# Mixture of experts by units of 256 rows, with the weights as stationary operand

## The chip, the cores and the metric

One core of a Trainium2 chip runs the kernel. The metric is device time in microseconds, the median of three runs: 465.23 us (462.66 to 465.39).

## The reference, cut to what matters

A cross attention with linear features, then a feed-forward mixture of eight experts, two for each row, over 2048 rows of 256 channels in fp32. The change touches the mixture alone.

```python
E, TOP_K, D, M = 8, 2, 256, 896
router_probs = softmax(layernorm(x) @ gate_w)
topk_w, topk_idx = top_k(router_probs, 2); topk_w /= sum(topk_w)
# rows sorted by expert, group_sizes rows for each of the 8
h = ragged_dot(rows, w1, group_sizes)                    # [n, 256] x [256, 896]
h = silu(h) * ragged_dot(rows, w3, group_sizes)
out_sort = ragged_dot(h, w2, group_sizes)                # [n, 896] x [896, 256]
x = x + sum over the two choices of topk_w * out_sort
```

## The kernel before, in words

**Attention, then the mixture.** The attention runs over eight pairs of 128 rows. Its last steps (`read`, `attend`, `project_attention`, the router of pairs 6 and 7) are interleaved with the mixture's first tiles. The router writes each normalised row twice, by an indirect DMA, into the `bucket` in HBM, a stretch of CAP rows for each expert, with its row number and weight behind it. The mixture then reads tiles of 128 rows from there.

**One tile.** (`mix` on the engines: L499, L855, L1082, L1339.) Each fp32 factor is held as two fp32r halves, and a product is hi*hi + hi*lo + lo*hi, so three matmuls. TensorE: `hidden` (L802) has the transposed rows as the stationary operand and streams 448 columns of the weights, 24 matmuls a tile for gate and up, in two halves c of the 896 channels; `x_transposes` (L783) turns the next tile's rows; `output` (L820) is the product with w2 of the tile before, 21 matmuls of 256 columns; `g_transposes` (L839) turns the gated channels, 7 of 128x128. ScalarE: `silus` (two of 448 columns), `evacuate_x`, `evacuate_y` (scaled by the row's weight), `load` (a register load of the row and the DMA of tile t+2), `high_g` (casts of the turned channels). VectorE: `gates` (product with the SiLU), `split_x`, `low_g` (the low halves). GpSimd: `add` (L489), an indirect DMA that adds the tile's rows to the output; each waits until the one before has landed.

**Weights.** w1, w3 and w2 of an expert are three DMAs of SyncE into one of two places of `raw`. In the first tile of expert e (table `tab_first`) the weights of e+1 are converted: `high_halves` (L1056) on ScalarE, three parts of two casts of 896 columns, and `low_part` (L485) on GpSimd, three subtractions. `expert_ready` counts experts and TensorE waits for it.

**Order of the tiles.** Four early tiles (`EARLY`, experts 0, 1, 1, 0) run before the counts are known. Then VectorE works out tables (which expert, which row, first of its expert, active or not) in small steps linked by `list_step` (L1445 to L1499), between its work for tiles 2 and 3. `tiles_of_mixture` (L198) runs tiles 5 to 7 written out, 8 to 31 in a loop of eight with a table value for the expert, and the rest under an If each. Engines read table values with `value_load`, a register load.

## Time and profile before

| | |
|---|---|
| three runs | 465.39, 462.66, 465.23 us |
| the profiled execution | 464.74 us, its span 463.0 us |
| granted TensorE clock, mean | 0.988 |
| busy: TensorE matmul, weight load | 428.7 us (93%), 396.0 us (86%) |
| busy: VectorE, ScalarE, GpSimd | 209.6 (45%), 230.9 (50%), 213.3 us (46%) |
| DMA | 46.1 MB, mean 100 GB/s |
| chain that ended last, by engine | PE 68%, DVE 9%, issue 6%, POOL 5%, DMA 4% |

The page tells busy shares of one execution. Starts of neighbouring instructions say more than their durations on TensorE, since matmuls overlap. Line numbers are those of the kernel above.

### The profile page before, as it was taken

Reading aid. Unit: us, or ns where it says so; the run is one execution under the profiler, and the core shown is the slowest. Engines: PE = TensorE matmul, PEld = TensorE weight load, DVE = VectorE, ACT = ScalarE, POOL = GpSimd, SP = SyncE. Lnnn points to the kernel's source line nnn. Section 1 sums busy time; section 2 is a strip of 40 time slices with the busy share of each in tenths; the row PEclk is TensorE's granted clock in tenths of the full one; section 3 lists DMA queues with packets and bytes.
Section 4 is the critical chain, followed back from the end, with each engine's and each line's share of the span. In section 5 each row is a group of like instructions: output and inputs, shape, how many; then the busy total and the mean of one; then the engine's idle time right before and its main releaser. Section 6 shows DMA issues by size and latency. Waiting matters only on the chain.

```text
span 463.0 us, 12218 instructions
## 1 busy us (share of the span) xinstructions
PE 428.7 (93%) x3921; PEld 396.0 (86%) x3922; DVE 209.6 (45%) x582; ACT 230.9 (50%) x477; POOL 213.3 (46%) x209
## 2 busy tenths in 40 slices
PE   3899999999999999989999998999999999999970
PEld 3789988898988888979999898899999899999970
DVE  4457788758876784323233331333232333233220
ACT  3677777578865523745333732553272373333320
POOL 4424375657434641798321671482177177121121
PEclk9999999999999999999999999899999999999996
DMA  8644121462128448335731236118121121121121
GB/s 255 195 134 156 47 70 48 145 234 70 49 59 286 114 128 260 80 122 168 256 54 24 37 110 187 23 35 272 23 43 29 23 39 30 23 46 23 36 37 11
DMA packets 34523, 46.10 MB, mean 100 GB/s; under 512 B 3488, under 2 KB 29344, under 8 KB 34464
## 3 DMA queue, kind: packets, MB, share of 16 engines
q1 hardware_dynamic: 22304, 31.82, 20.6%
q0 software_dynamic: 6576, 8.82, 11.3%
q10 hardware_dynamic: 5584, 4.76, 3.7%
q8 instruction: 27, 0.44, 0.4%
q14 instruction: 32, 0.26, 0.2%
HBM read 32.63 MB, written 12.76 MB: 98 GB/s over the span
## 4 chain that ended last, share of the span: by engine, by line
PE 68%; DVE 9%; issue 6%; POOL 5%; DMA 4%; ACT 2%; ACTq 1%; POOLq 1%; DVEq 0%
PE bank L814 28%; PE twin L833 15%; PE bank L852 4%; DMA out_rows<-qf,x_all 3%; POOL w_lo L486 3%; PE twin L667 3%; PE bank L547 3%; PE bank L548 2%; PE bank L549 2%; DVE w_lo L1229 2%; PE bank L593 2%; PE twin L679 2%; PE bank L571 2%; PE twin L792 1%; PE bank L610 1%
## 5 line engine op out<-in xcount | busy, mean ns | idle before, releaser
L496 POOL DMA_INDIRECT out_rows<-qf,x_all x35 | 54.6, 1559 | 147.4 <-ACT qf L1054 111.7
L814 PE MATMUL bank<-w_hi,c_hi 128*128 (+1 forms) x280 | 106.4, 380 | 3.8 <-issue 2.0
L814 PE MATMUL bank<-w_lo,c_hi 128*128 (+1 forms) x280 | 103.0, 368 | 0.0
L833 PE MATMUL twin<-w_hi,kv_halves 128*128 (+1 forms) x490 | 95.2, 286 | 2.9 <-DVE kv_halves L1335 2.4
L1329 DVE TENSOR_TENSOR x_all<-bank,x_all 128x448 f32<-128x448 f32 x70 | 43.4, 623 | 97.3 <-ACT x_all L1073 97.2
L486 POOL TENSOR_TENSOR w_lo<-raw,w_hi x18 | 76.0, 4422 | 12.8 <-ACT w_hi L1066 10.1
L1335 DVE TENSOR_TENSOR kv_halves<-bank,kv_halves 128x512 fp32r<-128x512 f32 x66 | 38.6, 623 | 93.9 <-ACT kv_halves L1078 93.9
L833 PEld LDWEIGHTS twin<-w_hi,kv_halves 128*128 128x128 f32 x490 | 77.5, 188 | 3.7 <-DVE kv_halves L1335 2.6
L814 PE MATMUL bank<-w_hi,c_lo 128*128 (+1 forms) x280 | 79.9, 367 | 0.0
L1073 ACT ACTIVATE x_all<-bank 128x448 f32<-128x448 f32 x70 | 37.8, 544 | 80.6 <-PE bank L814 70.1
L833 PE MATMUL twin<-w_lo,kv_halves 128*128 (+1 forms) x245 | 68.7, 280 | 0.0
L814 PEld LDWEIGHTS bank<-w_hi,c_hi 128*128 128x128 f32 x280 | 53.1, 190 | 9.6 <-issue 5.6
L814 PEld LDWEIGHTS bank<-w_hi,c_lo 128*128 128x128 f32 x280 | 52.9, 189 | 4.5
L814 PEld LDWEIGHTS bank<-w_lo,c_hi 128*128 128x128 f32 x280 | 53.3, 190 | 3.6
L1078 ACT CAST kv_halves<-bank 128x512 fp32r<-128x512 f32 x66 | 32.4, 540 | 29.6 <-PE bank L852 22.8
L1054 ACT ACTIVATE qf<-twin,x_all 128x256 f32<-128x256 f32 x35 | 16.6, 476 | 60.2 <-PE twin L833 60.2
L833 PEld LDWEIGHTS twin<-w_lo,kv_halves 128*128 128x128 f32 x245 | 46.3, 189 | 0.1
L428 POOL DMA_INDIRECT bucket<-rows,slot x32 | 36.8, 1150 | 16.2 <-DVE slot L1320 8.5
L852 PE MATMUL bank<-ident,x_all 128*128 128x128 f32 x233 | 32.4, 274 | 3.7 <-DVE x_all L1329 3.7
L1066 ACT CAST w_hi<-raw x36 | 32.0, 939 | 6.1 <-issue 4.3
L852 PEld LDWEIGHTS bank<-ident,x_all 128*128 128x128 f32 x233 | 26.2, 140 | 5.3 <-DVE x_all L1329 5.2
L379 POOL TENSOR_SCALAR rs<-mv 128x2 f32<-128x2 f32 (+2 forms) x12 | 2.8, 231 | 50.0 <-DVE mv L1193 33.7
(219 smaller groups left out, 703.4 us busy)
## 6 DMA issues: line engine op xcount, KB each, us to landing
raw<-in_w SPq DMA_DIRECT2D x24, 896.0 KB
x_all<-bucket ACTq DMA_DIRECT2D x31, 129.0 KB, 2.1
raw<-in_ctxT SPq DMA_DIRECT2D x8, 256.0 KB, 2.9
out_rows<-x_all SPq DMA_DIRECT2D x8, 256.0 KB, 2.1
bucket<-pad_rows SPq DMA_DIRECT2D x13, 129.0 KB, 2.4
x_all<-in_x SPq DMA_DIRECT2D x2, 512.0 KB, 6.4
x_all<-bucket SPq DMA_DIRECT2D x6, 129.0 KB, 2.7
x_all<-in_x SPq DMA_DIRECT2D x1, 768.0 KB, 6.3
```

Of the source, the lines that this page charges most:

```text
L428: pool.indirect_dma_start(out=bucket, out_offset=bass.IndirectOffsetOnAxis(ap=slot[:, o, k:k + 1], axis=0), in_=rows[i % 2][:, o, k, :], i ...
L486: return pool.tensor_tensor(w_lo[:, bass.ds(at + i * W13, W13)], raw[:, bass.ds(at + i * W13, W13)], w_hi[:, bass.ds(at + i * W13, W13)].b ...
L496: pool.indirect_dma_start(out=out, out_offset=bass.IndirectOffsetOnAxis(ap=x_in[:, v, D:D + 1].bitcast(U32), axis=0), in_=y[:, v, :], in_o ...
L814: last = nc.tensor.matmul(bank[b][:, 0:MC], stationary[:, k, :], w[:, bass.ds(at + (of + k * M + c * MC), MC)], start=(k == 0 and part == ...
L833: last = nc.tensor.matmul(bank[6][:, 0:D], stationary[:, k, :], w[:, bass.ds(at + (2 * W13 + k * D), D)], start=(k == 0 and part == 0 and ...
L852: last = nc.tensor.transpose(b[:, at:at + P], g[:, k * P:(k + 1) * P], ident[:])
L1054: nc.scalar.activation(y[:, v, :], bank[6][:, 0:D], ACT.Copy, scale=x_in[:, v, D + 1:ROW]).then_inc(y_ready, 1)
L1066: nc.scalar.copy(w_hi[:, bass.ds(at + of, PIECE)], raw[:, bass.ds(at + of, PIECE)]).then_inc(hi_ready, 1)
L1073: nc.scalar.activation(silu[:, c, :], bank[c][:, 0:MC], ACT.Silu).then_inc(silu_ready, 1)
L1078: nc.scalar.copy(g_hi[:, k:end, :].rearrange("p k n -> p (k n)"), b[:, 0:(end - k) * P]).then_inc(g_hi_ready, 1)
L1329: nc.vector.tensor_tensor(g[:, c * MC:(c + 1) * MC], bank[2 + c][:, 0:MC], silu[:, c, :], ALU.mult).then_inc(g_ready, 1)
L1335: nc.vector.tensor_tensor(g_lo[:, k:end, :].rearrange("p k n -> p (k n)"), b[:, 0:(end - k) * P], g_hi[:, k:end, :].rearrange("p k n -> p ...
```

## The change

A unit is now 256 rows, two tiles of 128 side by side (`o`), or a single tile where an expert has an odd number of tiles. The weights are the stationary operand: for each block c of 128 channels (7) `gate_up` gives gate and up for 256 rows, already with channels on the partitions, so nothing is turned. Both lie in one PSUM bank (`gate_bank(c)`, four in a ring). SiLU, product, cast and low half are made for each block, and `down` takes two row tiles of it as stationary operand, into one bank for y. In a single the moving operand is the high and the low half of the 128 rows side by side (256 columns), and VectorE adds the two results (`sums`). The early part has two units of two tiles. TensorE walks by expert: pairs under Ifs, from the fourth on in a loop, then the single under an If. The other engines walk units, all written out. x_in is one buffer, so row number and weight are copied out (`copy_meta`). `expert_ready` is split into `w13_ready` and `w2_ready`.

```diff
-EARLY = ((0, 0, 5), (1, 0, 5), (1, P, 5), (0, P, 6))
+TWO = 2 * P
+EARLY = ((1, 5), (0, 6))
-SURE = 2 * T // P
-MOST = SURE + E + AHEAD
-TILES = MOST + 2
+SURE = 2 * T // TWO
+MOST = SURE + E + 4
+UNITS = MOST + 2
+RING = 4
+UNITS_LISTED, ROWS_LISTED, ALL_LISTED = 6, 10, 14
...
+        def units_of_mixture(eng, step):
+            for t in range(AHEAD, SURE):
+                step(t)
+            def unit_if_used(t):
+                go = eng.value_load(tab_active[0:1, t:t + 1], min_val=0, max_val=1)
+                with eng.If(go):
+                    step(t)
+                    if t + 1 < MOST - 2:
+                        unit_if_used(t + 1)
+            unit_if_used(SURE)
...
+            sp.wait_ge(meta_ready, 2)
+            sp.dma_start(x_in[:, 0, :], bucket[TWO:TWO + P, :]).then_inc(x_in_loaded, 16)
+            sp.wait_ge(pad_stored[1], 16 * 2)
+            sp.wait_ge(list_ready, ROWS_LISTED)
+            at = sp.value_load(tab_row2[0:1, AHEAD:AHEAD + 1], min_val=0, max_val=PAD_AT)
+            sp.dma_start(x_in[:, 1, :], bucket[bass.ds(at, P), :]).then_inc(x_in_loaded, 16)
...
+                low_halves(0)
+                add_unit(t - 1, 0)
+                low_halves(1)
+                add_unit(t - 1, 1)
+                low_halves(2)
...
+            def gate_up(t, e, c, single=False):
+                if c == 0:
+                    pe.wait_ge(x_hi_ready, t + 1)
+                    pe.wait_ge(w13_ready, e + 1)
...
+                for i in range(2):
...
+                    if single:
+                        for k in range(KD):
+                            for w in (w_hi, w_lo):
+                                last = nc.tensor.matmul(out_ap, block(w, k), c_halves[:, :, k, 0:P],
+                                                        start=(k == 0 and w is w_hi), stop=(k == KD - 1 and w is w_lo))
+                        continue
+                    for k in range(KD):
+                        nc.tensor.matmul(out_ap, block(w_hi, k), x_hi[:, k, :], start=(k == 0), stop=False)
+                        nc.tensor.matmul(out_ap, block(w_lo, k), x_hi[:, k, :], start=False, stop=False)
...
+                    for k in range(KD):
+                        last = nc.tensor.matmul(out_ap, block(w_hi, k), x_lo[:, k, :], start=False, stop=(k == KD - 1))
+                last.then_inc(h_done, 1)
...
+            def unit(t, e, at_before, single=False):
...
+                gate_up(t, e, 0, single)
+                gate_up(t, e, 1, single)
+                down(t - 1, MB - 1, at_before)
+                gate_up(t, e, 2, single)
+                gate_up(t, e, 3, single)
+                first_down(t, e, tiles)
+                gate_up(t, e, 4, single)
+                down(t, 1, at, tiles)
+                x_transposes(t + 1)
+                gate_up(t, e, 5, single)
+                down(t, 2, at, tiles)
+                gate_up(t, e, 6, single)
+                for c in (3, 4, 5):
+                    down(t, c, at, tiles)
...
+            x_transposes(2)
+            down(1, 5, at1)
+            pe.wait_ge(list_ready, UNITS_LISTED)
+            for e in range(E):
+                of = e * NT + (3 if e < 2 else 1)
+                start = pe.value_load(tab_start[0:1, e:e + 1], min_val=AHEAD, max_val=MOST)
+                def pairs_if_listed(j):
+                    with pe.If(pe.value_load(tab_pairs[0:1, of + 2 * j:of + 2 * j + 1], min_val=0, max_val=1)):
+                        unit(start + j, e, (e if j else max(e - 1, 0)) % 2 * WALL)
+                        if j == 0:
+                            pairs_if_listed(1)
+                        else:
+                            with pe.If(pe.value_load(tab_pairs[0:1, of + 4:of + 5], min_val=0, max_val=1)):
+                                with pe.Fori(2, NT // 2 - (1 if e < 2 else 0)) as r:
+                                    with pe.If(pe.value_load(tab_pairs[0:1, bass.ds(2 * r + of, 1)], min_val=0, max_val=1)):
+                                        unit(start + r, e, e % 2 * WALL)
+                pairs_if_listed(0)
...
+            def load(t):
+                at = [act.value_load(tab[0:1, t:t + 1], min_val=0, max_val=PAD_AT) for tab in (tab_row, tab_row2)]
...
+                act.wait_ge(meta_ready, t)
+                for o in range(2):
+                    act.dma_start(x_in[:, o, :], bucket[bass.ds(at[o], P), :]).then_inc(x_in_loaded, 16)
...
+            def block_of(t, c):
+                silus(t, c)
+                high_g(t, c)
...
+            def mix(t):
+                first = None if t == AHEAD else act.value_load(tab_first[0:1, t:t + 1], min_val=0, max_val=1)
+                high_halves(first, t, 0)
+                block_of(t, 0)
+                block_of(t, 1)
+                evacuate_y(t - 1, (t - 1) % RING, (t - 1) % 2)
+                high_halves(first, t, 1)
+                block_of(t, 2)
+                block_of(t, 3)
+                high_halves(first, t, 2)
+                block_of(t, 4)
+                block_of(t, 5)
+                evacuate_x(t + 1)
+                block_of(t, 6)
+                copy_meta(t + 1)
+                if t == AHEAD:
+                    act.wait_ge(list_ready, ALL_LISTED)
+                    count.extend((units_used(act), last_places(act)))
+                load(t + 2)
...
+            def sums(t, c):
+                dve.wait_ge(h_done, MB * t + c + 1)
+                nc.vector.tensor_reduce(gate_bank(c)[:].rearrange("p (i k n) -> p i k n", i=2, k=2)[:, :, 0, :],
+                                        single_bank(c)[:].rearrange("p (i k n) -> p i n k", i=2, k=2), AX.X, ALU.add).then_inc(summed, 1)
...
+            def products(t, c, n=TWO):
+                dve.wait_ge(silu_ready, MB * t + c + 1)
+                nc.vector.tensor_tensor(product_in(c)[:, 0:n], product_in(c)[:, 0:n], silu[:, c % 2, 0:n], ALU.mult).then_inc(g_ready, 1)
...
+                with dve.If(single):
+                    sums(t, 0)
+                    for c in range(MB):
...
+                        products(t, c, P)
+                        if c + 1 < MB:
+                            sums(t, c + 1)
+                        low_g(t, c, P)
```

On ScalarE, before: the end of the second conversion in a tile (L1066 casts to w_hi), the second SiLU (L1073), the next tile's rows (L1048) and y (L1054).

```order
L1066 COPY w_hi<-raw 128x896
L1066 ISA
L1066 COPY w_hi<-raw 128x896
L1059 UNCONDITIONAL_BRANCH
L1073 ACTIVATE x_all<-bank 128x448 [waits h_done]
L1048 CAST c_hi<-twin 128x256 [waits xT_done]
L1054 ACTIVATE qf<-twin,x_all 128x256 [waits y_added,y_done]
L1034 TENSOR_LOAD kf
```

After: the end of the first conversion (L1127), then blocks 0 and 1 (L1136 SiLU, L1140 cast) and the two tiles of y (L1110).

```order
L1127 COPY w_hi<-raw 128x896
L1127 ISA
L1127 COPY w_hi<-raw 128x896
L1116 UNCONDITIONAL_BRANCH
L1136 ACTIVATE x_all<-bank 128x256 [waits summed,h_done]
L1140 CAST kv_halves<-bank 128x256 [waits g_ready]
L1136 ACTIVATE x_all<-bank 128x256 [waits summed,h_done]
L1140 CAST kv_halves<-bank 128x256 [waits g_ready]
L1110 ACTIVATE qf<-twin,meta 128x256 [waits y_added,y_done]
L1110 ACTIVATE qf<-twin,meta 128x256
```

A SiLU is no longer followed by a register load or by other work of the tile but by the cast of its own product, which waits for VectorE (g_ready). y of the unit before stands behind the first conversion and two blocks.

On ScalarE, before: the turned rows, y, then the register load of a row and its DMA, and the cast of g.

```order
L1048 CAST c_hi<-twin 128x256 [waits xT_done]
L1054 ACTIVATE qf<-twin,x_all 128x256 [waits y_added,y_done]
L1034 TENSOR_LOAD kf
L1034 ISA x2
L1041 ISA [waits y_added]
L1041 DMA x_all<-bucket 128x258
L1078 CAST kv_halves<-bank 128x512 [waits gT_done]
```

After, at the end of a unit: block 6, the row numbers, two register loads and two DMAs.

```order
L1136 ACTIVATE x_all<-bank 128x256 [waits summed,h_done]
L1140 CAST kv_halves<-bank 128x256 [waits g_ready]
L1103 COPY meta<-x_all 128x4 [waits y_added]
L1081 TENSOR_LOAD kf
L1081 ISA x2
L1081 TENSOR_LOAD kf
L1081 ISA x2
L1089 ISA [waits meta_ready]
L1089 DMA x_all<-bucket 128x258
L1089 ISA
L1089 DMA x_all<-bucket 128x258
```

The register load is doubled, and it stands between two units, with a short copy ahead of it.

On VectorE, before: the steps that give the row table (L1482), between two tiles' work.

```order
L1475 SCALAR_TENSOR_TENSOR n_tiles<-ends,cap_step 1x8
L1477 TENSOR_TENSOR qf<-qf,n_tiles 1x368 [waits list_step]
L1478 TENSOR_REDUCE kf<-qf 1x46 [waits list_step]
L1479 SCALAR_TENSOR_TENSOR kf<-tile_no,kf 1x46 [waits list_step]
L1481 TENSOR_SCALAR kf<-kf 1x46 [waits list_step]
L1482 CAST kf<-kf 1x46 [waits list_step]
L1329 TENSOR_TENSOR x_all<-bank,x_all 128x448 [waits silu_ready]
```

After: block 4 of unit 1 (L1406, L1410), the first row table (L1597) and the second (L1602).

```order
L1406 TENSOR_TENSOR bank<-bank,x_all 128x256 [waits silu_ready]
L1410 TENSOR_TENSOR kv_halves<-bank,kv_halves 128x256 [waits g_hi_ready]
L1590 SCALAR_TENSOR_TENSOR n_tiles<-ends,cap_step 1x8
L1592 TENSOR_TENSOR qf<-qf,n_tiles 1x240 [waits list_step]
L1593 TENSOR_REDUCE kf<-qf 1x30 [waits list_step]
L1594 SCALAR_TENSOR_TENSOR kf<-unit_no,kf 1x30 [waits list_step]
L1596 TENSOR_SCALAR kf<-kf 1x30 [waits list_step]
L1597 CAST kf<-kf 1x30 [waits list_step]
L1599 SCALAR_TENSOR_TENSOR kf<-kf 1x30
L1601 TENSOR_SCALAR kf<-kf 1x30 [waits list_step]
L1602 CAST kf<-kf 1x30 [waits list_step]
```

The list has three steps more here, and a block of unit 1 is set ahead of it, as ahead of every part of the list.

## Rows read from the trace of the kernel before

**Rows 1.** Busy time by stretch: us, busy us of each engine (x instructions), PEclk, DMA share, GB/s.
```profile
134.00:176.40 42.40, 39.70 (x342) 35.68 (x338) 30.77 (x121) 19.80 (x41) 21.18 (x29) 1.00 0.52 156
176.40:442.90 266.50, 260.33 (x1647) 244.05 (x1645) 84.14 (x158) 114.99 (x219) 119.55 (x49) 0.99 0.34 83
442.90:463.00 20.10, 6.41 (x52) 5.95 (x50) 2.11 (x4) 2.72 (x6) 3.10 (x2) 0.81 0.15 21
```
**Rows 2.** Groups by line: busy us, mean ns of one, then idle us before it.
```profile
L814 PE MATMUL bank<-w_hi,c_hi 128*128 (+1 forms) x280 | 106.4, 380 | 3.8 <-issue 2.0 <-POOL w_lo L486 1.6
...
L486 POOL TENSOR_TENSOR w_lo<-raw,w_hi x18 | 76.0, 4422 | 12.8 <-ACT w_hi L1066 10.1 <-DMA out_rows<-qf,x_all 2.7
...
L1066 ACT CAST w_hi<-raw x36 | 32.0, 939 | 6.1 <-issue 4.3 <-PE bank L814 0.8 <-DMA raw<-in_w 0.8
...
L1054 ACT ACTIVATE qf<-twin,x_all 128x256 f32<-128x256 f32 x35 | 16.6, 476 | 60.2 <-PE twin L833 60.2
...
L1324 DVE TENSOR_TENSOR c_lo<-twin,c_hi 128x256 fp32r<-128x256 f32 x34 | 14.1, 414 | 0.0
...
L1048 ACT CAST c_hi<-twin 128x256 fp32r<-128x256 f32 x34 | 12.5, 368 | 0.0
...
L1224 DVE TENSOR_TENSOR attT_lo<-twin,attT_hi 128x512 fp32r<-128x512 f32 x8 | 5.5, 692 | 7.9 <-ACT attT_hi L960 7.9
...
L960 ACT CAST attT_hi<-twin 128x512 fp32r<-128x512 f32 x8 | 4.7, 585 | 0.6 <-PE twin L703 0.6
```
**Rows 3.** Timeline of TensorE, one tile and the next start: start us, us, what.
```profile
331.67 0.38 PE L792 MATMUL twin<-ident,x_all 128*128 128x128 f32 x2
331.81 0.36 PE L833 MATMUL twin<-w_hi,kv_halves 128*128 x1
...
334.38 0.93 PE L852 MATMUL bank<-ident,x_all 128*128 128x128 f32 x7
335.07 0.45 PE L814 MATMUL bank<-w_hi,c_hi 128*128 x1
...
340.01 0.38 PE L792 MATMUL twin<-ident,x_all 128*128 128x128 f32 x2
...
348.74 0.38 PE L792 MATMUL twin<-ident,x_all 128*128 128x128 f32 x2
```
**Rows 4.** Timeline of ScalarE in the tile that converts weights.
```profile
335.82 0.97 ACT L1078 CAST kv_halves<-bank 128x512 fp32r<-128x512 f32 x2 [0.76 <-PE bank L852]
337.63 1.78 ACT L1066 CAST w_hi<-raw  x2 [0.84 <-issue]
339.32 0.53 ACT L1073 ACTIVATE x_all<-bank 128x448 f32<-128x448 f32 x1
339.75 1.77 ACT L1066 CAST w_hi<-raw  x2
```
**Rows 5.** Chain that ended last, ScalarE's register work: start us, us, what.
```profile
446.02 0.28 ACTq L1034
...
446.76 0.34 ACTq L1041
```
**Rows 6.** Timeline of VectorE, the list of tiles.
```profile
163.56 0.15 DVE L1457 CAST tab_count<-n_row 1x8 int32<-1x8 f32 x1
...
171.20 0.52 DVE L1478 TENSOR_REDUCE kf<-qf 1x46 f32<-1x368 f32 x1
...
172.20 0.18 DVE L1482 CAST kf<-kf 1x46 int32<-1x46 f32 x1
```
**Rows 7.** DMA issues: count, KB each, median us from issue to landing.
```profile
x_all<-bucket SPq DMA_DIRECT2D x6, 129.0 KB, 2.7
...
out_rows<-qf,x_all POOLq DMA_INDIRECT x35, 3.9
```
**Rows 8.** Chain that ended last, its last piece.
```profile
453.17 1.55 POOL out_rows L496
```
**Rows 9.** Timeline of ScalarE where its loop starts again.
```profile
288.40 0.98 ACT L1073 ACTIVATE x_all<-bank 128x448 f32<-128x448 f32 x2 [5.31 <-issue]
```

More of the change, by code:

```diff
@@ L831, in output, with down @@
+            def down(t, c, at, tiles=2):
+                pe.wait_ge(g_lo_ready, MB * t + (c + 1))
+                for o in range(tiles):
                     for part, stationary in enumerate((g_hi, g_lo)):
                         for w in ((w_hi, w_lo) if part == 0 else (w_hi,)):
-                            last = nc.tensor.matmul(bank[6][:, 0:D], stationary[:, k, :],
-                                                    w[:, bass.ds(at + (2 * W13 + k * D), D)],
-                                                    start=(k == 0 and part == 0 and w is w_hi),
-                                                    stop=(k == MB - 1 and part == 1))
@@ L855, in mix @@
-            def mix(t, u):
-                for c in range(2):
-                    hidden(t, c)
-                x_transposes(t + 1, (u + 1) % 4)
-                output(t - 1)
-                g_transposes(t)
-            x_transposes(0, 0)
+                            last = nc.tensor.matmul(bank[6][:, o * D:(o + 1) * D], stationary[:, c % RING, o * P:(o + 1) * P],
+                                                    w[:, bass.ds(at + (2 * W13 + c * D), D)],
+                                                    start=(c == 0 and o == 0 and part == 0 and w is w_hi),
+                                                    stop=(c == MB - 1 and o == 1 and part == 1))
@@ new lines, in down, with first_down @@
+                if c == MB - 1:
+                    last.then_inc(y_done, 1)
+            def first_down(t, e, tiles=2):
+                pe.wait_ge(w2_ready, e + 1)
+                if not isinstance(t, int) or t > 0:
+                    pe.wait_ge(y_ready, 2 * t)
+                down(t, 0, e % 2 * WALL, tiles)
+            def unit(t, e, at_before, single=False):
+                tiles = 1 if single else 2
+                at = e % 2 * WALL
+                gate_up(t, e, 0, single)
[12 more added lines that the diff above has]
+                    down(t, c, at, tiles)
@@ L900, in _ @@
-            output(n - 1, (E - 1) % 2 * WALL)
+            down(0, 4, at0)
+            down(0, 5, at0)
+            gate_up(1, e1, 0)
+            gate_up(1, e1, 1)
+            down(0, 6, at0)
+            gate_up(1, e1, 2)
+            rank(NPR - 1)
+            gate_up(1, e1, 3)
+            first_down(1, e1)
+            gate_up(1, e1, 4)
+            down(1, 1, at1)
+            gate_up(1, e1, 5)
+            down(1, 2, at1)
+            gate_up(1, e1, 6)
+            down(1, 3, at1)
+            down(1, 4, at1)
@@ L1057, in high_halves @@
+            def high_halves(first, t, part):
                 if first is None:
```

573 lines of the change are left out of this document (271 added, 302 removed).

## The prediction

> **What bounds the kernel now.** I read the page's busy shares first (TensorE 93%), then the busy time by stretch [rows 1], the groups by line [rows 2], and the timeline of one tile on TensorE and ScalarE. From 176.4 to 442.9 us TensorE works for 260 of 266.5 us. Every other engine there is under half busy (ScalarE 115, GpSimd 120, VectorE 84 us). In that stretch 31 tiles of the mixture run (35 in all, as L814's 280 matmuls of one group are 35 * 8 [rows 2]; four of them are earlier), 8.6 us each. One undisturbed tile takes 8.34 us from its L792 transposes to the next ones [rows 3]: 21 output matmuls of 256 columns in 331.81 to 334.38, 0.122 us each (0.118 between neighbours), 7 transposes in 0.69, and 24 matmuls of 448 columns in 335.07 to 340.01, 0.206 each (0.203 between neighbours). So TensorE's order is the bound, and ScalarE has room: per tile two SiLUs of 0.54, casts of 0.37 and 0.97, one row evacuation of 0.47 and one load, some 4 us of 8.3.
>
> **Which units there will be.** Routing the reference's own inputs gives the experts 346, 440, 686, 482, 636, 406, 592 and 508 rows (19 more for expert 0, moved by the early rows): 3, 4, 6, 4, 5, 4, 5 and 4 tiles, 35 as in the trace. In units of 256 that is 16 pairs and 3 singles (experts 0, 4, 6), 19 units: t = 0 and 1 early, t = 2 a single, then t = 3 to 18. Six of them (3, 4, 7, 9, 12, 14) also convert the next expert's weights.
>
> **TensorE alone.** A pair needs 84 gate/up and 42 down matmuls of 256 columns, 126 * 0.118 = 14.9 us, and 4 transposes of x, 0.35: 15.25 us. Two tiles take 16.65 now. What goes are the 14 transposes of g (1.4 us); 84 matmuls of 256 columns (9.9 us) cost what 48 of 448 do (9.7 to 9.9). A single needs 56 + 24 matmuls and the transposes, 9.8 us against 8.3, since the low half of x is multiplied by the low half of the weights too. 16 * 1.4 less, 3 * 1.5 more: 18 us less if nothing waits. I don't think that it is so, for two reasons.
>
> **ScalarE in a pair.** A channel block is now a chain of SiLU (256 columns: 0.38, from 0.54 at 448 by the 0.85 ns a column between the 256- and 512-column casts, 0.37 and 0.59 [rows 2]), product on VectorE (0.41), cast (0.37), with 0.03 from engine to engine; the next SiLU stands behind the cast in ScalarE's order. That is 1.17 us a block, 8.2 a unit. Beside it come the cast of x at 512 columns (0.59), two evacuations of y (0.86), the copy of the row numbers (0.2), and register work, for which the trace has the price: a register load and the DMA behind it run from 446.02 to 447.10, 0.5 us of it the load [rows 5], and nothing else goes on on ScalarE meanwhile. Two loads and two DMAs make 2.2 us, the table value of the unit 0.5. Sum 12.6 us of 15.25: no bound in a plain pair.
> In a unit that converts weights six casts of 0.94 are added [rows 2], in pairs of 1.7, and 0.9 of register loads before the first (between the second cast at 336.3 and L1066 at 337.63 lie 1.36 us [rows 4]). 18.9 us of ScalarE against 15.25 of TensorE: it becomes the bound. The schedule, from the unit's first gate matmul: last block of the unit before cast at 0.2, row loads to 2.4, conversion 3.75 to 5.5, blocks 0 and 1 to 7.8, y evacuated at 8.55. TensorE is at its first down block, which waits for that y, at 6.4: 2.2 us lost. The second conversion ends at 10.6, blocks 2 and 3 at 12.8, the third at 14.9, the low halves of blocks 4 and 5 come at 16.5 and 17.65, where TensorE would want them at 16.0 and 17.3: another 0.9. The unit takes 18.4 instead of 15.25. It leaves ScalarE 0.65 late, which the next unit pays in part (0.4). Before, the same conversion cost little (the tile in which it falls in [rows 3], 340.01 to 348.74, takes 8.73 instead of 8.34), since ScalarE had 4 us of a tile to spare. GpSimd's part, three subtractions of 4.4 us and two scatter-adds of 1.6, 16.4 us, I cost at nothing: the low halves of w1 and w3 are done some 16.5 us into the unit and wanted at 18.4, those of w2 at 22 and wanted at 18.4 + 6.4. If ScalarE had no part in it, GpSimd would allow no less than about 16.5.
>
> **A single** is bound by a ring: sum on VectorE (512 inputs, as the 512-column subtraction from PSUM of the trace, 0.69 [rows 2]), SiLU 0.38, product of 128 columns 0.28, next sum; 1.43 us a block with the ways. With the row loads ahead of it and y in the middle I come to 12.5 us against 9.8 on TensorE and 8.3 before. An operation of this kind on PSUM isn't in the trace; from below the ring is no bound (9.8), from above a sum at twice the price makes 17. I take 12.5.
>
> **The start.** The list of units is worked out on VectorE between the blocks of unit 1. Steps of it take 0.15 to 0.5 us each [rows 6]; in before the row table comes at 172.3, 8.8 us after the counts at 163.6, and its first user is a tile later. Now about 35 steps (9.5 us) and three blocks (1.25 each) stand between the counts and the second row table, 13.2 us. The counts come some 2 us later, as the blocks of unit 0 stand between the routing steps: 165.8 + 13.2 = 179. Unit 2 needs that table for its own rows (x_in is one buffer): 0.5 for the register, 2.7 to land [rows 7], transposes at 182.2, and 0.3 for them, 0.7 for the down block behind, and up to 2.7 for five register loads on TensorE, in part under it. Unit 2 starts at 184, where tile 4 started at 176.4. Bounds: 176 (the list hidden) to 187. TensorE idles about 5 us at one place there; the clock is 1.00 in this stretch now and 0.81 where it idles at the end [rows 1], so up to 2 us at a lower clock may come on top.
>
> **The sum.** From 184: three singles 37.7; converting units 6 * 18.4 = 110.4, with 0.65 more for t = 4 and 12 and 3.1 for t = 3 (behind a single, and five register loads once on ScalarE, 2.5) 114.8; pairs behind a late ScalarE 6 * 15.65 = 93.9; two plain ones 30.5; less 2.1, as the last unit's down blocks belong to the tail. 274.8. The tail from the end of the last gate matmuls is 20.1 now (442.9 to 463.0). The scatter-add starts at 453.17 [rows 8], 10.25 after them. Now the first starts at about +6.6 (down block 6, y, and the same 0.9 of branches on GpSimd), but the second waits until the first has landed, 3.9 [rows 7] and 0.5: +11. 20.9 in all. The span is 184 + 274.8 + 20.9 = 479.7. The profiled execution took 464.74 for a span of 463.0, 0.5 below the median of 465.23: 481.4 by the one, 481.9 by the other. I say 481.
>
> **Rivals.** *Register work lies beside the casts.* If ScalarE fetched registers while it computes, a converting unit would lose 0.5 instead of 3.15: 16 us, and 4 at t = 3 and behind late units: 461. For it: in [rows 4] the SiLU at 339.32 and the pair of casts at 339.75 follow one another without a gap, so a SiLU of 0.53 covers one load. Against it: the 1.36 and 1.1 us of [rows 4, 5], where nothing stood ahead to cover them.
> *TensorE's order decides, and nothing waits*: start at 176.4, 14 * 15.25 + 29.4 - 2.1, tail and way: 440. It needs the chain of casts to be hidden in the converting units; all sums on ScalarE speak against it.
> *Far jumps on TensorE (slower still).* The mixture on TensorE is now code by expert: three pair bodies (one in a loop), one single, each jumped over when not listed, and expert 2 walks its loop five times for nothing. On ScalarE the trace shows what the way back of the old loop cost: 5.31 us of "issue" before L1073 at 288.40 [rows 9]. On TensorE no such gap is to be seen at its own way back, as its queue was full. With twelve jumps and ten ways (there and back) in that loop, each costing 5.3 less some 3.8 of work in its queue (32 matmuls of 0.118, an estimate of how far it runs ahead, from the old loop that shows no gap), 33 us: 514. From zero to that; it decides from jumps whose target isn't loaded. The Trainium skill, "Runtime: NRT & Kernel Launch", "Instruction fetch mechanics", says that fetching ahead is sequential only and a taken branch outside of the window stalls for a fetch. By that rule these jumps would cost as here reckoned; the trace agrees on ScalarE (5.31 us) and shows nothing of it on TensorE. ScalarE's own loop is unrolled now, so that stall is in none of my sums for after.
>
> **How the numbers follow.** My forecast 0.5 (own range 471 to 491), register work hidden 0.2, nothing waits 0.12, jumps 0.13, and 0.05 between. A change of under 1% is about what a measurement of this kernel can't tell, 460.6 to 469.9. The 461 case falls half into faster. So faster 0.21, same 0.14, slower 0.65. The range 450 to 497 leaves out most of the 440 case and the upper end of the jumps.
>
> **What would show it.** Right: ScalarE busy or in register work without a pause in units 3, 4, 7, 9, 12, 14; TensorE idle 2 to 2.5 us before the first down block there, released by y; these units 18 to 19 us apart and plain ones 15.3 to 15.7; singles at 12 to 13; a gap of about 5 us before the x transposes of unit 2, released by a DMA; two scatter-adds 4.4 us apart at the end. Wrong: converting units at 15.5 us, or "issue" gaps of several us on TensorE at expert changes.

## The result, and the profile after

The changed kernel takes 519.9 us (median of 6 runs, 515.4 to 523.6) where the kernel before takes 466.45 beside it (462.7 to 470.0): a ratio of 1.114, 95% interval 1.107 to 1.122. The forecast was 481, with a range to 497. The direction was right, the size was not. The profiled execution has a span of 516.7 us.

From the page of the kernel after: the busy shares, the granted clock by slice, a queue that fetches instructions (packets, MB) and the chain that ended last:
```profile
PE 432.2 (84%) x4365; PEld 414.0 (80%) x4366; DVE 244.8 (47%) x732; ACT 254.5 (49%) x609; POOL 217.0 (42%) x211
...
PEclk9999999999999858887999699799999979889975
...
q8 instruction: 49, 0.80, 0.7%
...
PE 63%; DVE 15%; issue 10%; ACT 6%; ACTq 2%; DMA 2%; POOL 1%; SPq 0%; POOLq 0%; DVEq 0%
```
TensorE was 93% busy before and is 84% busy now, and no other engine has taken its place: none is at half. So the time is in pauses of TensorE. A tenth of the chain is "issue", time in which the engine waited for nothing that the profile shows. The same by stretch, cut at the x transposes of unit 2, the first gate matmul of unit 3 and the end of the mixture's steady part (columns as in [rows 1]):
```profile
...
180.70:203.60 22.90, 14.88 (x95) 14.17 (x95) 10.63 (x34) 7.21 (x20) 3.10 (x2) 0.72 0.56 161
203.60:488.70 285.10, 248.89 (x1937) 245.46 (x1938) 103.83 (x248) 129.35 (x317) 121.07 (x49) 0.92 0.30 70
...
```
In its steady stretch TensorE of before was idle 6 of 266.5 us at a clock of 0.99 [rows 1]. Here it is idle 36 of 285, at 0.92. What it idles for stands in the view of its waits (us in total, times, longest):
```profile
PE bank L832 <- issue: 29.2, 8, 10.2
PE bank L828 <- issue: 9.2, 4, 6.1
...
PE bank L801 <- DMA x_all<-bucket: 4.4, 1, 4.4
PE twin L846 <- DVE kv_halves L1410: 4.3, 5, 2.4
PE twin L846 <- ACT qf L1110: 3.8, 3, 2.3
PE twin L846 <- issue: 2.9, 1, 2.9
```
41.3 us are "issue"; my forecast's wait for y (ACT qf L1110) is 3.8. The timeline of TensorE says where. These are all its issue pauses of over 2 us (start us, us, what, and in brackets the idle time before it):
```profile
189.23 0.57 PE L828 MATMUL bank<-c_halves,w_hi 128*128 128x256 f32 x1 [6.13 <-issue]
...
234.93 0.55 PE L832 MATMUL bank<-c_halves,w_hi 128*128 128x256 f32 x1 [10.17 <-issue]
235.28 0.42 PE L833 MATMUL bank<-c_halves,w_lo 128*128 128x256 f32 x1
235.50 0.41 PE L832 MATMUL bank<-c_halves,w_hi 128*128 128x256 f32 x1
...
290.70 0.55 PE L832 MATMUL bank<-c_halves,w_hi 128*128 128x256 f32 x1 [7.82 <-issue]
...
328.10 0.55 PE L832 MATMUL bank<-c_halves,w_hi 128*128 128x256 f32 x1 [4.03 <-issue]
...
412.93 0.55 PE L832 MATMUL bank<-c_halves,w_hi 128*128 128x256 f32 x1 [3.53 <-issue]
...
497.84 0.57 PE L846 MATMUL twin<-w_hi,kv_halves 128*128 128x256 f32 x1 [2.88 <-issue]
```
Each is the first matmul behind code that was jumped over: the pair bodies of expert 0 (189.23); expert 1's second pair, its loop and its single body (234.93); five empty turns of expert 2's loop and its single (290.70); the loop and single of experts 3, 5 and 7 (328.10, 412.93, 497.84). Where an expert ended in a single, nothing lay between and the pause is 1.0 to 1.3 us. The same 1.3 us stand ahead of the singles of experts 4 and 6 (at 362.84 and 447.94), where one body, that of the loop, was jumped over. Behind the long pauses the matmuls start 0.21 to 0.22 us apart (235.28, 235.50) instead of 0.118, and the granted clock there is 0.5: TensorE comes back at the lower clock level.

That 234.93 is no wait for data is seen on the timelines of ScalarE and GpSimd. ScalarE cast x of unit 4 at 222.7, and GpSimd's last low half of expert 2's weights ended at 222.17 + 4.56 = 226.7:
```profile
222.74 0.59 ACT L1096 CAST c_halves<-bank 128x512 fp32r<-128x512 f32 x1
...
227.98 1.78 ACT L1127 CAST w_hi<-raw  x2 [3.08 <-issue]
```
```profile
222.17 4.56 POOL L488 TENSOR_TENSOR w_lo<-raw,w_hi  x1
```
The casts at 227.98 convert the next expert's weights in unit 4, whose first matmul comes 7 us after them.

### The profile page after: what moved, and what is told of

The parts are those of the page before. It is cut to its first block, busy times and chain, and to the rows that moved or that the text cites. A ratio compares the mean times of both kernels' runs of the same rounds, so it can differ in the third digit from the quotient of the medians.

```text
span 516.7 us, 12140 instructions
## 1 busy us (share of the span) xinstructions
PE 432.2 (84%) x4365; PEld 414.0 (80%) x4366; DVE 244.8 (47%) x732; ACT 254.5 (49%) x609; POOL 217.0 (42%) x211
## 4 chain that ended last, share of the span: by engine, by line
PE 63%; DVE 15%; issue 10%; ACT 6%; ACTq 2%; DMA 2%; POOL 1%; SPq 0%; POOLq 0%; DVEq 0%
PE twin L846 13%; PE bank L832 9%; PE bank L833 9%; PE bank L837 9%; PE twin L677 3%; PE bank L557 3%; DVE bank L1406 2%; PE bank L558 2%; PE bank L559 2%; DVE w_lo L1299 2%; PE twin L689 2%; PE bank L603 2%; PE bank L828 1%; PE bank L581 1%; DVE bank L1401 1%
## 5 line engine op out<-in xcount | busy, mean ns | idle before, releaser
L832 PE MATMUL bank<-c_halves,w_hi 128*128 128x256 f32 x448 | 125.8, 300 | 29.2 <-issue 29.2
L498 POOL DMA_INDIRECT out_rows<-qf,meta x38 | 59.2, 1557 | 160.0 <-ACT qf L1110 111.2
L833 PE MATMUL bank<-c_halves,w_lo 128*128 128x256 f32 x448 | 123.2, 295 | 0.0
L846 PE MATMUL twin<-w_hi,kv_halves 128*128 128x256 f32 x496 | 109.3, 289 | 11.1 <-DVE kv_halves L1410 4.3
L832 PEld LDWEIGHTS bank<-c_halves,w_hi 128*128 128x128 f32 x448 | 90.9, 203 | 30.7 <-issue 30.6
L1406 DVE TENSOR_TENSOR bank<-bank,x_all 128x256 f32<-128x256 f32 (+1 forms) x133 | 54.2, 407 | 128.0 <-ACT x_all L1136 127.8
L837 PE MATMUL bank<-c_halves,w_hi 128*128 128x256 f32 x448 | 94.6, 294 | 0.0
L1136 ACT ACTIVATE x_all<-bank 128x256 f32<-128x256 f32 x133 | 51.5, 387 | 81.5 <-PE bank L837 46.8
L833 PEld LDWEIGHTS bank<-c_halves,w_lo 128*128 128x128 f32 x448 | 91.3, 204 | 0.0
L1140 ACT CAST kv_halves<-bank 128x256 fp32r<-128x256 f32 x133 | 49.5, 373 | 81.2 <-DVE bank L1406 81.2
L1410 DVE TENSOR_TENSOR kv_halves<-bank,kv_halves 128x256 fp32r<-128x256 f32 (+1 forms) x133 | 53.5, 402 | 49.6 <-ACT kv_halves L1140 49.6
L837 PEld LDWEIGHTS bank<-c_halves,w_hi 128*128 128x128 f32 x448 | 74.3, 204 | 0.0
L846 PE MATMUL twin<-w_lo,kv_halves 128*128 128x256 f32 x248 | 71.0, 286 | 0.0
L430 POOL DMA_INDIRECT bucket<-rows,slot x32 | 37.0, 1156 | 23.0 <-DVE slot L1392 15.6
L1127 ACT CAST w_hi<-raw x36 | 32.1, 938 | 24.3 <-issue 15.6
L828 PE MATMUL bank<-c_halves,w_hi 128*128 128x256 f32 x48 | 13.1, 303 | 8.7 <-issue 8.7
```

The source lines that it names most:

```text
L430: pool.indirect_dma_start(out=bucket, out_offset=bass.IndirectOffsetOnAxis(ap=slot[:, o, k:k + 1], axis=0), in_=rows[i % 2][:, o, k, :], i ...
L498: pool.indirect_dma_start(out=out, out_offset=bass.IndirectOffsetOnAxis(ap=meta[:, v, o, 0:1].bitcast(U32), axis=0), in_=y[:, u, o, :], in ...
L832: nc.tensor.matmul(out_ap, block(w_hi, k), x_hi[:, k, :], start=(k == 0), stop=False)
L833: nc.tensor.matmul(out_ap, block(w_lo, k), x_hi[:, k, :], start=False, stop=False)
L837: last = nc.tensor.matmul(out_ap, block(w_hi, k), x_lo[:, k, :], start=False, stop=(k == KD - 1))
L846: last = nc.tensor.matmul(bank[6][:, o * D:(o + 1) * D], stationary[:, c % RING, o * P:(o + 1) * P], w[:, bass.ds(at + (2 * W13 + c * D), D)],
```

## The experiments

The kernel before ran beside each group of versions, so versions of different groups are compared by their ratio to it (466 us, 1% is 4.7 us).

| version | median us | ratio to before (95%) |
|---|---|---|
| after | 519.9 | 1.114 (1.107 to 1.122) |
| TensorE's units written out | 492.0 | 1.050 (1.043 to 1.058) |
| the same, register loads put back | 495.4 | 1.058 (1.052 to 1.064) |
| written out, y first | 486.8 | 1.045 (1.041 to 1.049) |
| and second row of unit 2 known | 481.3 | 1.034 (1.031 to 1.037) |
| and singles as pairs | 490.5 | 1.044 (1.040 to 1.049) |
| and no conversion on ScalarE | 471.6 | 1.008 (1.004 to 1.011) |
| after, y first | 518.3 | 1.115 (1.110 to 1.119) |
| before, loops written out | 466.5 | 0.995 (0.991 to 0.998) |

**1. No branches on TensorE.**
```diff
-            for e in range(E):
-                start = pe.value_load(tab_start[0:1, e:e + 1], min_val=AHEAD, max_val=MOST)
...
-                pairs_if_listed(0)
-                with pe.If(pe.value_load(tab_odd[0:1, e:e + 1], min_val=0, max_val=1)):
...
+            LIST = ((2, 0, True), (3, 1, False), (4, 2, False), (5, 2, False), (6, 2, False), (7, 3, False),
...
+            for t, e, single in LIST:
+                unit(t, e, was % 2 * WALL, single)
+                was = e
```


> The kernel after, but TensorE's nineteen units are written out in the order of these inputs' list: its expert walk has no branch, no loop and no register load, and its numbers are constants. The other engines are unchanged and still read their lists. Left out is only that TensorE would follow another list. JUMPS (the eleven issue gaps of TensorE, some 38 us in sum, are its branches over bodies that don't run): all gaps of over 1 us called issue at the expert changes vanish; the clock, 0.92 from 203.6 us on, comes back to 0.97 or more; 470 to 485 us, since ScalarE's evacuation in the converting units shows once the gaps no longer cover it. SCALARE (my forecast: the converting units are bound by ScalarE whatever TensorE does): the units 3, 4, 7, 9, 12 and 14 still take 18.4 us or more each, so not under 479. DATA (the gaps are waits for weights or rows that the profile does not name): the same stretches come back as waits, time over 505.


Measured 492.0 us, clock 0.96 over all. (In this kernel, the next one and the first one with skips, the last down block of unit 1 takes its weights from the place of expert 1 where expert 0's are due; the number of matmuls is the same.) The stretches from the start of unit 2 on, and the waits of TensorE:
```profile
184.40:204.00 19.60, 17.10 (x119) 16.46 (x120) 10.47 (x33) 7.09 (x20) 3.10 (x2) 0.82 0.65 182
204.00:476.00 272.00, 243.76 (x1971) 238.20 (x1970) 106.31 (x254) 131.54 (x326) 122.91 (x51) 0.99 0.31 74
```
```profile
PE twin L846 <- ACT qf L1094: 16.4, 7, 5.4
...
PE twin L846 <- DVE kv_halves L1394: 6.2, 12, 2.9
...
PE twin L846 <- issue: 2.4, 5, 0.8
```
The pauses at the expert changes are gone, and the clock is back at 0.99. The third theory (data) falls. But 41.3 - 2.4 = 38.9 us of issue went and the span fell by 26.1: the wait for y (ACT qf) rose from 3.8 to 16.4, that for low halves (DVE kv_halves) from 4.3 to 6.2. So 14.5 us of the pauses had covered work of ScalarE and VectorE, which shows now; so does a wait of 1.8 us for VectorE at unit 2. The time is 7 us above the top of what the first theory expected, and the second theory's bound (not under 479) holds too: both mechanisms are real, and in the kernel after the one hides the other.

**2. The register loads alone.** 47 loads of table values put back between the units, values unused:
```diff
+                    pe.value_load(tab_start[0:1, e:e + 1], min_val=AHEAD, max_val=MOST)
...
+                    pe.value_load(tab_pairs[0:1, e * NT:e * NT + 1], min_val=0, max_val=1)
```


> The kernel before this one in the call (units written out, constants), with 47 register loads of TensorE from its lists put back where the expert walk has them, their values unused; no branch. JUMPS: within 5 us of the version without loads, gaps at the changes of 0.3 to 1.3 us (as the after trace shows where a change has no skipped body: 1.04 to 1.32). LOADS (register loads, not branches, drain TensorE): gaps of 3 to 10 us are back, 500 us or more.


```profile
PE bank L832 <- issue: 10.3, 8, 2.3
PE twin L846 <- ACT qf L1108: 7.8, 5, 1.9
```
3.4 us more than without them (the intervals of the two ratios overlap), gaps of 0.7 to 1.4 us and one of 2.3, and less waiting for y, as they cover part of it. Loads do not make the large pauses. That leaves the branches.

**3. What a branch costs.** In the written-out kernel, bodies that never run stand ahead of units that convert nothing.
```diff
+            def skip(t, e, bodies):
+                with pe.If(pe.value_load(tab_single[0:1, 3:4], min_val=0, max_val=1)):
+                    for i in range(bodies):
+                        unit(t, e, e % 2 * WALL)
...
+            SKIPPED = {5: (1,), 6: (2,), 8: (3,), 10: (1, 1), 13: "turns", 15: (2, 1), 18: (1, 1, 1)}
```


> Units written out, constants, no loads but these: ahead of unit 5 a branch over one unit body that never runs (some 105 instructions), ahead of 6 over two bodies, ahead of 8 over three, ahead of 10 two branches over one each, ahead of 13 a loop of five turns each of which skips one body, ahead of 15 a branch over two and one over one, ahead of 18 three branches over one each. None is a converting unit, so nothing else is late there. FIXED PRICE (each taken branch to code not yet fetched costs about 3.5 to 4 us whatever its length): 3.5, 3.5, 3.5, 7, for 13 7 or more, 7, 10.5 us. DISTANCE (the price follows what is skipped): one body under 2 us, two about twice, three three times, and 18 no more than 8. LOADS ONLY (branches are free, the load before them costs): all of them about 0.5 us per load.


One run, 535.0 us, with the unit order of the list above; TensorE's pauses:
```profile
247.08 0.36 PE L832 MATMUL bank<-c_halves,w_hi 128*128 128x256 f32 x1 [0.52 <-issue]
...
265.19 0.36 PE L832 MATMUL bank<-c_halves,w_hi 128*128 128x256 f32 x1 [2.47 <-issue]
...
304.68 0.55 PE L832 MATMUL bank<-c_halves,w_hi 128*128 128x256 f32 x1 [4.07 <-issue]
...
344.72 0.55 PE L832 MATMUL bank<-c_halves,w_hi 128*128 128x256 f32 x1 [3.60 <-issue]
...
399.01 0.55 PE L832 MATMUL bank<-c_halves,w_hi 128*128 128x256 f32 x1 [6.03 <-issue]
...
441.77 0.55 PE L832 MATMUL bank<-c_halves,w_hi 128*128 128x256 f32 x1 [7.46 <-issue]
...
494.83 0.55 PE L832 MATMUL bank<-c_halves,w_hi 128*128 128x256 f32 x1 [5.78 <-issue]
```
None of the three theories holds alone. A price per branch would make the first 3.5; distance alone would make two and one (7.46) equal to three (4.07). The pauses sum to 29.9 us, the span is 42.6 us above that of the written-out kernel: TensorE's busy time for the same matmuls is 11.6 us longer (435.4 against 423.8), at the lower level behind the pauses. The same with the places exchanged:
```diff
-            SKIPPED = {5: (1,), 6: (2,), 8: (3,), 10: (1, 1), 13: "turns", 15: (2, 1), 18: (1, 1, 1)}
+            SKIPPED = {5: (3,), 6: (1,), 8: (2,), 10: (2, 1), 13: (1, 1, 1), 15: (1, 1), 18: "turns"}
```


> The skip experiment with its places exchanged, to see which of its sizes hold: three bodies ahead of unit 5 (were 4.07 us), one ahead of 6 (0.52), two ahead of 8 (2.47), two and one ahead of 10 (7.46), three times one ahead of 13 (5.78), twice one ahead of 15 (3.60), the loop of five turns ahead of 18 (6.03). DISTANCE AND COUNT: each size comes back within 1 us at its new place. PLACE (what happens to be fetched or loading there decides): sizes change by 2 us or more, while three bodies still cost more than one.


```profile
246.55 0.55 PE L832 MATMUL bank<-c_halves,w_hi 128*128 128x256 f32 x1 [3.67 <-issue]
...
301.73 0.36 PE L832 MATMUL bank<-c_halves,w_hi 128*128 128x256 f32 x1 [3.54 <-issue]
...
347.18 0.55 PE L832 MATMUL bank<-c_halves,w_hi 128*128 128x256 f32 x1 [9.86 <-issue]
...
403.00 0.55 PE L832 MATMUL bank<-c_halves,w_hi 128*128 128x256 f32 x1 [7.13 <-issue]
...
443.38 0.55 PE L832 MATMUL bank<-c_halves,w_hi 128*128 128x256 f32 x1 [3.88 <-issue]
...
494.43 0.55 PE L832 MATMUL bank<-c_halves,w_hi 128*128 128x256 f32 x1 [4.55 <-issue]
```
The places are three bodies, (one: no pause of 0.3 us or more), two, two and one, three times one, twice one, the five turns. Neither theory holds alone: four of the seven sizes come back within 1.1 us, two move by 1.4 and 1.5, one by 2.4. Their order mostly holds: one body 0 to 0.5, two 2.5 and 3.5, three 3.7 and 4.1, one and one 3.6 and 3.9, three times one 5.8 and 7.1, two and one 7.5 and 9.9, the empty loop 4.6 and 6.0. Hence, in these two runs: a single jump over one body costs nearly nothing, a longer one 2.5 to 4 us, and a second branch right behind the first costs about 3 us or more even over one body (3.1 to 3.9 behind a jump over one, 5.0 and 6.3 behind a jump over two). The changed kernel has just that: the branch over the pairs and, right behind it, the one over the single.

The Trainium skill, "Runtime: NRT & Kernel Launch", "Instruction fetch mechanics", says that instructions are fetched in blocks of 256, ahead in sequence only, with two blocks in the window, and that a taken branch out of it waits for a fetch. A body is 130 matmuls, each with its weight load, about one block (the expectation's 105 instructions were too few), so by that rule one body is free and two are not; both traces agree (0 to 0.5 us, then 2.5 and 3.5). For TensorE the same section also gives room for 2048 instructions; with eight blocks in the window none of these jumps would leave it, and the traces decide against that. It says nothing of two branches in a row. The instruction queue agrees that more is fetched: 49 packets of 16 KB here and in the kernel after, 34 in the written-out kernel.

**4. A version for any list, with short branches.** Each unit stands twice on TensorE, for even and for odd experts; singles run as pairs.
```diff
+                with pe.If(even):
+                    unit(t, e, at_before, at=0)
+                with pe.If(odd):
+                    unit(t, e, at_before, at=WALL)
```


> A version for any list without far branches: TensorE walks the units by their number, and each unit stands twice, once for even and once for odd experts, the one not wanted being branched over (one body, some 105 instructions; unit 5 of the skip experiment paid 0.5 us for one body, two branches in a row over one each 3.6). Singles run as pairs with pad rows on all engines (TensorE's three singles so cost about 5.4 us more each, 11 over all as unit 2 also waits). DISTANCE: 17 skips at 0.5 to 1 us, so 492 plus 9 to 17 plus 11 to 16: 512 to 525. PRICE PER BRANCH (a body that runs also ends in a branch, so two for each unit at about 2 us or more): 555 or more.


```profile
PE bank L832 <- issue: 23.6, 14, 5.4
```
513.1 us in one run, so near the lower end of "distance": most pauses at a change of unit are 0.8 to 1.5 us (two register loads among them). Only where an even expert ends do two skips follow one another, and there 2.2, 4.9, 1.6 and 5.4 us are lost. By the ratio of this one run (1.104) it is 5 us under the kernel after, though its singles cost more; a single run doesn't settle that.

**5. ScalarE's order.** Evacuate y ahead of the weight conversion:
```diff
-                high_halves(first, t, 0)
                 block_of(t, 0)
                 block_of(t, 1)
                 evacuate_y(t - 1, (t - 1) % RING, (t - 1) % 2)
+                high_halves(first, t, 0)
                 high_halves(first, t, 1)
```


> TensorE's units written out with constants as in the first experiment (whose last down of unit 1 also read its weights at the place of expert 1 instead of expert 0; mended here), and on ScalarE the evacuation of the unit before stands ahead of the first piece of the weight conversion instead of behind it. The first experiment measured 492.0 us, with seven waits of TensorE for this evacuation, 16.4 us in sum, in the converting units and unit 3. SCALARE'S ORDER: those waits fall to under 4 us in sum, and the time to 476 to 482. SCALARE'S LOAD (the engine has no room in a converting unit, wherever its work stands): the waits come back as waits for gate or product values further on in the same units, and the time stays within 4 us of 492.


```profile
PE twin L846 <- DVE kv_halves L1394: 14.9, 18, 2.6
...
PE twin L846 <- ACT qf L1094: 4.5, 2, 2.9
```
The wait for y fell from 16.4 to 4.5 us, that for the low halves rose from 6.2 to 14.9. The ratio fell by 0.5 of a percent, inside the intervals. So it is ScalarE's load in a converting unit more than its order, as the second theory said. With the branches still there the same edit must then give nothing:


> The kernel after, branches and all, with ScalarE's evacuation ahead of the conversion and nothing else. If the branch gaps cover ScalarE's work in the converting units, as the after trace suggests (waits for the evacuation only 2.3, 0.6 and 0.9 us), the move is worth 2 to 4 us: 516 to 518. If ScalarE were the bound beside the gaps, as my forecast had it, it would be worth 15 or more: under 505.


The ratio is 1.115 where the kernel after has 1.114: nothing that can be measured. The pauses cover ScalarE, as the first theory had it, and its 2 to 4 us did not show.

**6. The start.** On top of 5, without the wait for the second row table:
```diff
-            sp.wait_ge(list_ready, ROWS_LISTED)
-            at = sp.value_load(tab_row2[0:1, AHEAD:AHEAD + 1], min_val=0, max_val=PAD_AT)
-            sp.dma_start(x_in[:, 1, :], bucket[bass.ds(at, P), :]).then_inc(x_in_loaded, 16)
+            sp.dma_start(x_in[:, 1, :], bucket[PAD_AT:PAD_AT + P, :]).then_inc(x_in_loaded, 16)
```


> The kernel before this one in the call, and SyncE loads the second tile of unit 2 from the pad rows without waiting for the list (in these inputs' list unit 2 is a single; another list would not be followed). ROW TABLE: TensorE's wait for the rows of unit 2, 3.8 to 4.4 us, goes, and the time falls by 3 to 4 us. LIST ON VECTORE: the list steps still hold the first products of unit 2, the wait moves to them, and less than 1.5 us is gained.


5.5 us less in the same group, slightly more than the wait for the rows, which is gone; the first theory holds. What is left there is 2.6 us for VectorE, which comes to x of unit 2 only after its last list steps:
```profile
184.12 0.55 PE L826 MATMUL bank<-c_halves,w_hi 128*128 128x256 f32 x1 [2.59 <-DVEq L1602]
```

**7. What the singles give.** On top of 6, the three singles as pairs (`True` becomes `False` in LIST, and VectorE runs every unit as a pair).


> The kernel of the known second row (481.3 us: TensorE's units written out, ScalarE's evacuation ahead of the conversion, the second tile of unit 2 from the pad rows), with the three singles run as pairs whose second tile is pad rows, on TensorE and VectorE. TENSORE'S WORK decides the singles: three times 15.3 less 9.8, 16 us more: 496 to 499. RING decides them (the chain of PSUM, ScalarE and VectorE takes 12.4 to 14.7 us for a single as for a pair, as the distances between the row transposes of that run show): 5 to 9 us more, 486 to 490.


The ratio rises from 1.034 to 1.044, 4.9 us: the ring theory, at its lower end. The three singles together save 5 us, not the 16 that their matmuls would. The timeline of VectorE in a single of experiment 8's kernel shows the ring, two sums with a product and a low half between them:
```profile
331.18 0.69 DVE L1383 TENSOR_REDUCE bank<-twin 128x256 f32<-128x512 f32 x1
...
332.58 0.69 DVE L1383 TENSOR_REDUCE bank<-bank 128x256 f32<-128x512 f32 x1
```
From sum to sum it is 1.40 us, where I had reckoned 1.43.

**8. No conversion on ScalarE.** On top of 6, the high halves of experts 2 to 7 are not made, their semaphore is counted on:
```diff
-                        nc.scalar.copy(w_hi[:, bass.ds(at + of, PIECE)], raw[:, bass.ds(at + of, PIECE)]).then_inc(hi_ready, 1)
+                        act.sem_inc(hi_ready, 1)
```


> The kernel of the known second row (481.3 us), with ScalarE's copies of the high halves of experts 2 to 7's weights left out (36 of its casts less the twelve of experts 0 and 1; their semaphore is still counted), so that part of the computation is missing. SCALARE'S LOAD: the waits of TensorE in the converting units (1.3 to 1.6 us each named after VectorE, and the smaller ones around them) vanish, 8 to 12 us less: 469 to 473. ORDER OR RING (the waits come from the order of blocks or the four places of the ring, and the conversion only coincides): within 3 us of 481.


The ratio falls from 1.034 to 1.008, 12.3 us:
```profile
PE twin L844 <- DVE kv_halves L1392: 5.1, 5, 3.2
```
From unit 5 to 15 pairs lie 15.4 us apart now (one 15.6), converting units too (in the kernel after only plain pairs did). So ScalarE's load cost 12 us. Even then, without branches, row-table wait and conversion, the new mixture is no faster than the old.

**9. The old kernel without its loops.** Tiles 8 to 31 written out on every engine, then nested branches:
```diff
-            with eng.Fori(1, SURE // 8) as r:
-                for i in range(8):
-                    step(8 * r + i, i % 4)
+            for t in range(8, SURE):
+                step(t, t % 4)
```


> The kernel before, with its two loops over tiles written out on every engine (tiles 8 to 31 straight, from 32 on nested branches), same work. Its ScalarE has issue gaps of 5.31 and 4.99 us where the loop turns, its TensorE idles at most 1.7 us there. LOOP TURNS COST: 2 to 5 us less, 0.5 to 1% under the kernel before. HIDDEN: TensorE had work queued, no difference that can be measured.


Ratio 0.9945 (0.9914 to 0.9977), 2.6 us less, the same work. ScalarE's "issue" in front of its SiLU, 10.3 us in two pauses (one is [rows 9]), is gone from its waits, and with it TensorE's wait of 1.7 us for VectorE at the turn. In exchange TensorE has an "issue" pause of 3.0 us (at 450.89) among the last tile's output matmuls, where the nested branches are left. Half a percent under the kernel before is clear of the noise here, but small.

## Why the prediction was wrong, point by point

*The step that failed is the far jumps.* I left them out of the sum and kept them as a rival with a chance of 0.13, because TensorE showed no "issue" gap of that size at the way back of the old loop (0.5 us at 291.32, and 1.7 us of waiting for VectorE ahead of it). "Issue" gaps at expert changes were the sign of being wrong that I had named, and they came. In the rival's own terms they are 33 us and 514; measured are 41.3 us of issue pauses, which cost 28 us, and 520. That 514 comes so near is in part luck: 22 jumps at one price of 1.5 us were reckoned, and what came were six pauses of 2.9 to 10.2 us and five of 1.0 to 1.3. The reason against them was read wrongly: the missing gap showed that one way back was covered, not that two branches in a row would be. For that the trace had no row, and the rival's rule, a price of each jump less the work queued, should have stood in the sum at least by half. Its count was wrong too: jumps over one body are nearly free, and what costs are longer ones and the second of two.

*ScalarE in the converting units: right in mechanism and size, but hidden.* The written-out kernel is the case I forecast. From first gate matmul to first gate matmul its converting unit 7 takes 18.28 us and the plain unit behind it 15.47, where I had 18.4 and 15.65:
```profile
274.05 0.28 PE L832 MATMUL bank<-c_halves,w_hi 128*128 128x256 f32 x1
...
292.33 0.28 PE L832 MATMUL bank<-c_halves,w_hi 128*128 128x256 f32 x1
...
307.80 0.28 PE L832 MATMUL bank<-c_halves,w_hi 128*128 128x256 f32 x1
```
Units 9 and 14 take 18.25, unit 12, behind a single, 19.05 (19.05). The waits for y in the six converting units sum to 14.7 us where I had 16.3. The kernel has 492 us, 11 above my 481: unit 2 starts at 188.5 instead of 184 (that execution came to the x transposes of unit 1 3 us later than the one of after, and VectorE's last list steps held x for 1.8, which I had not), and from there to the end it takes 302.1 instead of 295.7. Unit 2 itself took the forecast 12.6, at a clock of 0.82. The terms that were too small are unit 3 (2.1 us: its wait for y was 5.4, as reckoned, but the matmuls behind that wait ran at the lower level), unit 17 (1.7, a wait for y behind 4.0 us of "issue" on ScalarE), unit 18 (0.9) and the tail (2.8, below); the others were 1.2 too large in sum.

*TensorE alone.* Right: a plain pair takes 15.42 us (15.25). But "18 us less if nothing waits" was never to be had, since the singles are bound by their ring (12.3 to 13.0 us in the written-out kernel, forecast 12.5) and not by the 9.8 us of their matmuls: experiments 7 and 8.

*The start.* The counts came at 165.3 (165.8) and the second row table at 177.5 (179), the transposes at 180.7 (182.2), after 4.4 us idle (5):
```profile
165.31 0.15 DVE L1552 CAST tab_count<-n_row 1x8 int32<-1x8 f32 x1
...
177.54 0.17 DVE L1602 CAST kf<-kf 1x30 int32<-1x30 f32 x1
```
Unit 2's first matmul, forecast at 184, came at 189.2, behind the first far jump (6.1 us, of which the written-out kernel still has 1.8 as a wait for VectorE).

*The tail: a jump on ScalarE that I had at nothing.* I wrote that ScalarE's loop is unrolled, so that no such stall is in my sums. But ScalarE's units from 19 on stand under nested branches, and leaving them is a jump over seven bodies, with the branches to the last unit's y behind it. From the end of the last gate matmul (492.7) to 516.7 are 24.0 us, forecast 20.9; the two scatter-adds are 4.6 us apart (4.4), and come 2.8 and 3.0 later than forecast:
```profile
500.76 0.84 ACT L1110 ACTIVATE qf<-twin,meta 128x256 f32<-128x256 f32 x2 [5.67 <-issue]
```
```profile
502.14 1.55 POOL L498 DMA_INDIRECT out_rows<-qf,meta  x1 [10.58 <-ACT qf L1110]
506.71 1.55 POOL L498 DMA_INDIRECT out_rows<-qf,meta  x1 [3.02 <-DMA out_rows<-qf,meta]
```
TensorE's own last pause (2.9 us at 497.84) does not explain it: the written-out kernel has no pause there and a tail of 23.7. There TensorE's last matmul ends at 470.6 and ScalarE's last two DMA issues at 470.8, but y is evacuated only at 474.6:
```profile
474.56 0.84 ACT L1094 ACTIVATE qf<-twin,meta 128x256 f32<-128x256 f32 x2 [5.33 <-issue]
```
In experiment 8's kernel that pause is 7.3 us. The kernel before had none: its last y waited for TensorE. No version without these branches on ScalarE was run, so that they are the cause is read from the code and the traces, not shown by an experiment.

*The other rivals.* "Register work beside the casts" (461) and "nothing waits" (440) are out: even the kernel without conversion is at 471.6.

Put together from the ratios, the 11.4% are: 6.4 the branches, net of what they cover; 0.5 ScalarE's order (not certain); 1.1 the second row table; 2.6 the conversion; 0.8 what is left. The shares hold for this order of removal.

## What to carry to other kernels

Code laid out by case, with bodies jumped over, is paid on the engine that is the bound: count the taken branches there, and above all those that follow one another with nothing executed between, as the second costs some 3 us or more here. Count them too on the engine that hands over the last result: a way out of unused units stands in the tail. A covered jump in the old trace says nothing of a new one whose queue is empty. And when a pause and a loaded engine meet in the same unit, removing one shows the other: undo them one after the other before giving each its share.

## What the runs showed of the hardware

That a jump over one unit body (130 matmuls with their weight loads) costs 0 to 0.5 us, but two such in a row 3.6 to 3.9, I had not expected; nor that an empty loop of five turns, 4.6 to 6.0, costs no more than two or three plain branches. In the kernel after TensorE came back from the pauses of 2.88 us and more at 0.21 to 0.22 us a matmul, the lower level (granted clock 0.5), for a while. Behind pauses of 1.0 to 1.3 us it was mixed: at 362.84 and 375.83 it went on at its 0.12, at 203.59 it came back at 0.21, and at 447.94 and 462.14 it began at 0.12 and fell to 0.21 some 1 to 1.6 us later. So it is not the length of the last pause alone: in the second skip experiment a pause of 3.54 us was followed by 0.12 for 1.3 us and 0.21 only then, one of 3.67 by 0.21 at once. The written-out kernel has a clock of 0.99 in its steady stretch against 0.92. What that is worth can be read from TensorE's busy time for the same 4365 matmuls, 432.2 us in the kernel after and 423.8 written out: 8.4 of the 26.1 us of span are slower matmuls, 17.7 are idle time (the written-out execution was 3 us later before the first of these pauses). Why the same skip costs up to 2.4 us more or less at another place, and why two in a row lost 1.6 to 5.4 in experiment 4, stays open.
